# Decoder layer on one core: first batches of the self-attention phase reordered, query-weight low parts moved from VectorE to GpSimd

## What is computed

```python
x = _layernorm(x + self_attention(x))            # causal, 16 heads of 32; q = x @ w_q.T, k = x @ w_k.T, v = x @ w_v.T, out @ w_o.T
x = _layernorm(x + cross_attention(x, context))  # 361 context rows, 16 query heads of 128, 4 key heads, RMS norm of q and k
x = _layernorm(x + mixture(x))                   # top 2 of 8 experts, silu, projection, RMS norm
```

## Time and profile before

| | |
|---|---|
| median of 3 runs | 1489.28 us (1487.9 to 1490.34) |
| the profiled execution, its time | 1489.16 us |
| its span, first to last instruction | 1487.4 us |
| mean granted TensorE clock | 0.977 of full speed |
| PE busy | 1393.6 us (94%) |
| weight loads busy (PEld) | 1176.0 us (79%) |
| DVE busy | 851.4 us (57%) |
| ACT busy | 710.0 us (48%) |
| POOL busy | 594.2 us (40%) |

### The profile page before, as it was taken

One profiled execution on the slowest core, in us unless ns is written; L12 is line 12 of the kernel. 1 busy time (PEld: TensorE's weight loads), 2 busy tenths in 40 slices (PEclk: granted clock), 3 DMA queues, 4 the chain that ended last, 5 costly groups with the idle time before them and its releaser, 6 DMA issues. The chain is left out here.

```text
span 1487.4 us, 24718 instructions
## 1 busy us (share of the span) xinstructions
PE 1393.6 (94%) x8497; PEld 1176.0 (79%) x8497; DVE 851.4 (57%) x3018; ACT 710.0 (48%) x1877; POOL 594.2 (40%) x936
## 2 busy tenths in 40 slices
PE   7889999999987999999999999999999998399996
PEld 6778888887876788888888888888888887277874
DVE  3654343434346676667666765765676665843457
ACT  3655555556325454444444444444454446243346
POOL 1222111212115445455545544554445446264074
PEclk9999999999998999999999999999999999699999
DMA  6211121212443221221222121212221213485372
GB/s 201 91 34 58 56 73 52 79 34 68 142 127 103 76 56 48 65 60 37 67 60 58 35 76 49 68 37 65 59 59 46 65 39 108 175 247 162 114 252 102
DMA packets 70547, 126.56 MB, mean 85 GB/s; under 512 B 11835, under 2 KB 47007, under 8 KB 69528
## 3 DMA queue, kind: packets, MB, share of 16 engines
q1 hardware_dynamic: 65848, 110.04, 24.3%
q0 software_dynamic: 4576, 14.95, 3.6%
HBM read 93.50 MB, written 31.45 MB: 84 GB/s over the span
## 5 line engine op out<-in xcount | busy, mean ns | idle before, releaser
L1363 POOL TENSOR_TENSOR b_pcarry<-b_half 128x1 f32<-128x1 f32 x173 | 43.0, 249 | 364.6 <-DVE b_rinv L1226 343.1
L76 PE MATMUL bank<-b_kTh,b_q 128*100 128x362 f32 x512 | 173.6, 340 | 8.3 <-POOL b_q L1384 5.7
L1106 ACT ACTIVATE b_probs<-b_probs,b_nmax 100x361 f32<-100x361 f32 x256 | 152.4, 595 | 54.7 <-DVE b_nmax L1220 54.6
L1220 DVE CUSTOM_DVE_ANT_0 b_probs<-bank,b_mask 100x361 f32<-100x361 f32 x256 | 135.5, 529 | 69.9 <-issue 61.3
L1395 POOL TENSOR_SCALAR b_probs<-b_probs,b_rinv 100x361 f32<-100x361 f32 x256 | 152.6, 609 | 0.0
L1101 ACT ACTIVATE b_pTh<-bank 121x400 fp32r<-121x400 f32 x192 | 96.1, 501 | 85.1 <-PE bank L937 83.7
L1213 DVE TENSOR_TENSOR b_pTl<-bank,b_pTh 121x400 fp32r<-121x400 f32 x192 | 109.6, 571 | 44.2 <-ACT b_pTh L1101 44.2
L1157 ACT ACTIVATE b_oTh<-bank,b_bv 128x400 fp32r<-128x400 f32 x64 | 38.1, 596 | 198.6 <-PE bank L76 198.6
L937 PE MATMUL bank<-ident,b_probs 100*121 100x100 f32 x768 | 111.7, 268 | 4.1 <-POOL b_probs L1395 3.4
L937 PEld LDWEIGHTS bank<-ident,b_probs 100*121 100x121 f32 x768 | 107.7, 187 | 8.0 <-POOL b_probs L1395 4.4
L436 ACT ACTIVATE a_probs<-a_probs,a_nmax 100x100 f32<-100x100 f32 x256 | 93.1, 366 | 40.3 <-DVE a_nmax L555 40.3
(11 more groups left out here) (256 smaller groups left out, 3818.7 us busy)
## 6 DMA issues: line engine op xcount, KB each, us to landing
q_d<-a_qb SPq DMA_DIRECT2D x64, 200.0 KB, 2.3
b_q_raw<-q_d SPq DMA_DIRECT2D x64, 200.0 KB, 2.4
b_q_raw<-rs_d SPq DMA_DIRECT2D x64, 200.0 KB, 3.4
b_ctxr<-in_ctxT SPq DMA_DIRECT2D x48, 242.0 KB, 4.5
y_d<-c_y SPq DMA_DIRECT2D x32, 256.0 KB, 3.5
c_Eraw<-in_expert_w SPq DMA_DIRECT2D x10, 512.0 KB, 7.8
a_stage<-in_Wq SPq DMA_DIRECT2D x4, 1024.0 KB, 4.9
stage<-in_Wo SPq DMA_DIRECT2D x8, 512.0 KB, 4.5
```

Of the source, the lines that this page charges most:

```text
L76: mm = eng.matmul(out, lhsT=l(c), rhs=r(c), start=first and k == 0, stop=last and k == n - 1)
L1106: act.activation(p, p, ACT.Exp, scale=-1.0, bias=nmax[:, s % 2, h:h + 1], accum_out=psums[:, s % 2, h:h + 1]).then_inc(e_rdy, 1)
L1220: dve.tensor_tensor_reduce(out=probs[:, s % 2, h, 0:SE], in0=s_bank[h % 2][0:S, 0:SE], in1=mask_s[:], scale=-1.0, scalar=BIG, op0=ALU.add, ...
L1363: pool.tensor_tensor(pcarry[:, k:k + 1], half_s[:, 0:1], half_s[:, 0:1], ALU.add)
```

## The change

- The projection for the next pair is cut up in the first batches. In batches 1 to 4 its first half stands ahead of the transposes of x1; in batches 0 to 3 its last quarter stands behind the transposes of the probabilities.
- At the start ACT writes both halves of the scaled queries ahead of the high part of w_o; DVE writes the low part of w_o behind the first masks.
- Each of batches 0 to 3 gets one Wq piece: its high part on ACT (batch 0: behind the output's high part; batches 1 to 3: between the exponentials and x1's high part), its low part on GpSimd at the end of the batch, with a semaphore of its own (wq_lo).
- In even batches before 4, DVE copies the first half of the keys ahead of its copies of the transposed probabilities and the second half behind them.
- wk and wq are laid out in DRAM and SBUF by quarters, so a quarter is one run of 2 KB in each partition; the causal mask is loaded behind both.

```diff
 SQ = 5
-WQ_SPLITS = ((), (2,), (3, 4), (5,))
 KV_FRAME, CTX_FRAME = (50, 52, 59, 61), (48, 50, 57)
...
 
-        wq_s = sb("a_wq", [P, DC, D])
-        wk_s = sb("a_wk", [P, DC, D])
+        wq_s = sb("a_wq", [P, DC, DC, P])
+        wk_s = sb("a_wk", [P, DC, DC, P])
         wvh, wvl = sb("a_wvh", [P, DC, D], F32R), sb("a_wvl", [P, DC, D], F32R)
...
         consts, w_raw, w_hi, w_lo = sem("a_consts"), [sem("a_w_raw0"), sem("a_w_raw1")], sem("a_w_hi"), sem("a_w_lo")
+        wq_lo = sem("a_wq_lo")
         wq_in, wk_in = [[sem(f"a_{w}_in{m}") for m in range(DC)] for w in ("wq", "wk")]
...
             sp.dma_start(xTr[:], xT[0]).then_inc(xT_in, 16)
-            sp.dma_start(causal_s[:], causal).then_inc(causal_in, 16)
             for dst, src, loaded in ((wk_s, w_k, wk_in), (wq_s, w_q, wq_in)):
                 for m in range(DC):
-                    sp.dma_start(dst[:, :, m * P:(m + 1) * P], src[:, :, m * P:(m + 1) * P]).then_inc(loaded[m], 16)
+                    sp.dma_start(dst[:, m], src[:, m]).then_inc(loaded[m], 16)
+            sp.dma_start(causal_s[:], causal).then_inc(causal_in, 16)
             sp.dma_start(qkw_s[:, 0:1], qn_w).then_inc(consts, 16)
...
                 for n in ((2, 3), (4,), (5,))[i] if i < 3 else ():
-                    sp.wait_ge(w_lo, n - 1)
+                    sp.wait_ge(w_lo if n < 4 else wq_lo, (n - 2) % 2 + 1)
                     sp.dma_start(stage[:, n % 2], pieces[n][0]).then_inc(w_raw[n % 2], 16)
...
                         mm = pe.matmul(p_bank(pair, is_q, m // 2)[:, m % 2 * 2 * S:(m % 2 + 1) * 2 * S],
-                                       lhsT=w[:, c, m * P:(m + 1) * P], rhs=xTr[:, c, :], start=c == 0, stop=c == DC - 1)
+                                       lhsT=w[:, m, c, :], rhs=xTr[:, c, :], start=c == 0, stop=c == DC - 1)
                     if m % 2:
...
                 if group == 0 and m % XG == 0:
-                    pe.wait_ge(w_lo, 3 + kv)
+                    pe.wait_ge(wq_lo, 1 + kv)
                 if m >= 2:
...
                 if 1 <= i <= GB:
+                    project(pair + 1, (wk_s, wq_s)[par], range(2), (wk_in, wq_in)[par])
                     transpose_x1(i - 1)
-                if pair + 1 < NPAIR:
-                    project(pair + 1, (wk_s, wq_s)[par], range(DC), (wk_in, wq_in)[par])
+                    project(pair + 1, (wk_s, wq_s)[par], range(2, 3 if i < GB else DC), (wk_in, wq_in)[par])
+                elif pair + 1 < NPAIR:
+                    project(pair + 1, (wk_s, wq_s)[par], range(3 if i < GB else DC), (wk_in, wq_in)[par])
                 elif m[1] is not None:
...
                     mm.then_inc(pt_done, 1)
+                if i < GB:
+                    project(pair + 1, (wk_s, wq_s)[par], range(3, DC), (wk_in, wq_in)[par])
                 if m[2] is not None:
...
                 if b == GB:
-                    act.wait_ge(w_lo, len(pieces))
+                    act.wait_ge(wq_lo, len(pieces) - 2)
                 if b % GB == 0 and b >= 2 * GB:
...
             scaled_q(0, 0)
+            scaled_q(0, 1)
             split_hi(1)
-            scaled_q(0, 1)
             act.wait_ge(half_set, 3)
...
                 exponent(i, 3)
+                if 1 <= i < GB:
+                    split_hi(2 + i)
                 if 1 <= i <= GB:
...
                 act.activation(v_s[:], bank[7][0:S, :], ACT.Copy).then_inc(v_ev, 1)
-                for n in WQ_SPLITS[i] if i < GB else ():
-                    split_hi(n)
                 if i >= GB and par == 1 and pair + 1 < NPAIR:
...
                 act.activation(oTh[:].rearrange("p c t -> p (c t)"), bank[7][:, 0:DC * S], ACT.Copy).then_inc(oT_hi, 1)
+                if i == 0:
+                    split_hi(2)
                 head_squares(m[2])
...
                 if m == 0:
-                    dve.wait_ge(w_lo, len(pieces))
+                    dve.wait_ge(wq_lo, len(pieces) - 2)
                 if m % XG == 0:
...
             split_lo(0)
-            split_lo(1)
-            dve.wait_ge(bq_in, 16)
-            dve.wait_ge(qkw_set, 2)
             for i in range(B):
...
                 elif i == 0:
+                    split_lo(1)
                     invert_sums(i, 0)
...
                     invert_sums(i, 2)
+                    dve.wait_ge(bq_in, 16)
+                    dve.wait_ge(qkw_set, 2)
                 else:
...
                 if i < GB:
-                    for n in WQ_SPLITS[i]:
-                        split_lo(n)
+                    if par == 0:
+                        dve.wait_ge(ks_ev, pair + 1)
+                        copy_k(pair + 1, 0)
                     probs_T(i, 1)
                     probs_T(i, 3)
+                    if par == 0:
+                        copy_k(pair + 1, 1)
                 queries(m[1])
...
                                   oTh[:].bitcast(F32).rearrange("p c t -> p (c t)"), ALU.subtract).then_inc(oT_lo, 1)
-                if pair + 1 < NPAIR:
-                    if par == 0:
-                        if i < GB:
-                            dve.wait_ge(ks_ev, pair + 1)
-                            copy_k(pair + 1, 0)
-                            copy_k(pair + 1, 1)
-                    else:
-                        split_xT(pair + 1)
+                if par == 1 and pair + 1 < NPAIR:
+                    split_xT(pair + 1)
                 queries(m[3])
...
                                    ALU.mult).then_inc(pn_rdy, 1)
+
+            def query_weights_lo(n):
+                pool.wait_ge(w_hi, n + 1)
+                pool.tensor_tensor(pieces[n][2], stage[:, n % 2], pieces[n][1].bitcast(F32), ALU.subtract).then_inc(wq_lo, 1)
 
...
                     keys_in_place(pair + 1)
+                if i < GB:
+                    query_weights_lo(2 + i)
             t = TAIL
...
 
+    def by_output(w):
+
+        return w.reshape(P, w.shape[1], w.shape[2] // P, P).transpose(0, 2, 1, 3)
+
     a = {k: np.asarray(v) for k, v in inputs.items()}
...
         "xT": x.reshape(B // 2, 2, S, DC, P).transpose(0, 4, 3, 1, 2).reshape(B // 2, P, DC, 2 * S),
-        "w_q": chunks(a["L0_attn_w_q"].T),
-        "w_k": chunks(a["L0_attn_w_k"].T),
+        "w_q": by_output(chunks(a["L0_attn_w_q"].T)),
+        "w_k": by_output(chunks(a["L0_attn_w_k"].T)),
         "w_v": chunks(a["L0_attn_w_v"].T),
...
         "Wq": a["L0_xattn_Wq"].reshape(DC, P, XKV, XG * XHD).transpose(2, 1, 0, 3),
```

## The result

The changed kernel took 1477.07 us (median; 1474.73 to 1479.81) beside 1488.59 us (1484.82 to 1490.45) for the kernel before on the same chip: a ratio of 0.9927, interval 0.9905 to 0.9949, or 11.5 us less. The forecast was 1476.7. Three of the six executions took 1474.73 to 1474.86 us with a mean granted clock of 0.980, three took 1479.27 to 1479.81 with 0.976 to 0.977, so the median lies where no execution did.

What follows compares the result with a forecast made beforehand. TensorE was busy nearly throughout, so its waits and half-clock stretches up to batch 4 counted; gains of 4.0 + 2.1 + 2.7 + 2.4 + 1.3 = 12.5 us off 1489.2 gave 1476.7, range 1472.5 to 1482.

Steps and rivals of the forecast that it cites:

- The start: Start to batch 0's product of probabilities and values: that product begins at 30.5 instead of 34.46, gain 4.0 us, bounds 1.9 and 5.3.
- From W: Batch 0, W being w_v's landing at 15.6: scores start near W + 2.9, product of probabilities and values at W + 14.9.
- The 1.0 us put down to the layout: Start: 2 KB runs for wk and wq let w_v land 1.0 us earlier, at 15.6 instead of 16.6.
- The cuts: Batches 1 to 4: cut projections cover PE's waits for x1 and the probability copies; gains 2.1, 2.7, 2.4 and 1.3 us.
- was hidden under the projection and gives nothing: Later batches: taking the 2.3 us query-weight subtraction off DVE saves no time, since the projection already covered it.
- GpSimd's subtraction: End of batches 0 to 3: a query weight's low part takes 4.8 us, bounds 4.4 and 5.6; first ends 8.1 into its step.
- The low part of xT: DVE in batches 1 and 3: beside GpSimd's subtraction this 0.99 us operation ends 1.0 to 1.5 us late, 1.3 taken.
- Rival A: Batches 2 and 4: no conflict between DVE's low part of xT and GpSimd; 1.8 us more gain, 1474.9 us; 15%.
- Rival B: Softmax chain, with ACT's split in it, ends the batches; PE waits 1 us more in three, 1479.7 us; 20%.
- Rival C: Half clock stays at the start and recurs in batches 1 to 4 or later, 1.7 us each; 1479.3 to 1481; 15%.
- Rival D: GpSimd's subtraction holds up every batch's first normalisation in full, 19.2 us against 12.5; slower, 1495.9 us; 3%.
- Rival E: PE's holes only move to the last normalisation, with no net gain over 3 us; 3%.

Runs made afterwards that it cites:

- the two warm-up kernels: Twelve unused 128x128 products ahead of the first projection: on the changed kernel 1477.4 us; with the second and fourth query-weight subtractions also on DVE 1473.53 us.
- the last kernels: Changed kernel with warm-up products, second and fourth subtractions on DVE, ACT's split behind x1's high part: 1475.93 us; also w_v loaded earlier, w_o split later: 1470.43 us.

## Why the prediction was right, and where it was off

**The sum.** 12.5 us were forecast, 12.29 measured at batch 4 and 11.5 between the medians; the time came within 0.4 us. That is luck in two ways. Two errors cancel, the start too high by 1.2 and the steps too low by 1.0; and the median fell between two groups of executions, 2.2 us to either side of it, so no execution came within 1.8 us of the forecast.

**The start was over-priced: 4.0, measured 2.84** (T0 31.62, said to be 30 to 31). Part of this is scatter: the same start gave 2.8 to 3.6 in five kernels, and its order alone, on the old layout, gave 4.03. The step that went wrong is "From W": it let w_v's arrival set the scores' start at W + 2.9. The link itself holds (T0 = W + 14.9 was the forecast, and where w_v is last, as in the two warm-up kernels, it measures 14.75 and 14.76). W came at 15.17, earlier than my 15.6, which by that link gives 30.1. But PE's own two projections ended only at 19.45, and T0 followed 12.17 behind them, the same to 0.02 in the two kernels with the odd subtractions moved (18.65 to 30.82, 19.28 to 31.46) and in that with ACT's split behind x1 (19.40 to 31.58). I had taken PE's end for given because before its projections were over 3.16 us ahead of the scores; I had not asked why the first of them took 7.39 us where the second takes 5.58. By its pace it began at the lower clock, and in after that cost 2.7 us (8.28). With the start's order alone PE's projections ended at 18.32, and there T0 = W + 14.91 (15.52, 30.43), as the forecast's chain has it. The 1.0 us put down to the layout was never there: W scatters from 15.2 to 16.7 with either layout.

**The cuts were right, and under-priced by 0.3, 0.1, 0.3 and 0.2.** T0 to T1 took 15.36 (15.7 forecast), T2 to T3 15.10 (15.4). The waits that I had added in batch 1 (0.3) did not come, and PE's own work in batches 2 and 3 is 15.1 instead of 15.4, as the last kernels' steps show (batch 1's is 15.4). Batch 4's 14.19 was 14.4 in the forecast. No wait stands before L385, as said. What the prediction does not say, and the two halves run alone show, is that neither cuts nor move give more than 0.9 us in the steps by themselves: the sum of terms was right only for both together. That DVE's 2.3 us a piece "was hidden under the projection and gives nothing" held only as long as the projection stood there whole: with the cuts alone it is 8.8 us of waits.

**GpSimd's subtraction**: 4.54 to 4.63 us, 4.8 forecast; the first ended at T0 + 8.0 (39.60 - 31.62), as said.

**The low part of xT**: over 2 us in batches 1 and 3, as said (2.18 each time). It lost 1.19 of the 1.34 us that the two had in common (49.23 to 50.57), where I took 1.3 lost. The Trainium skill, "SBUF — State Buffer", section "Who interferes with whom", would have the second wait for the whole of the first, 1.34 lost: the trace agrees to 0.15 us, and is nearer to it than to the two thirds of the earlier trace rows. Batch 2's step was 16.83 for a forecast of 17.0, with 0.94 us before the fourth transposes (1.2 forecast) and 0.40 before x1's (under 0.7, as said).

**Rival A**, no conflict, falls by the row of 2.18 us. Its price was 1.8; taking the conflict away in fact gave 1.19 in batch 2 and 0.34 in batch 4 (0.61 with the subtraction on DVE). **Rival B**, the softmax chain, was at work in batch 2 alone: moving ACT's split gave back 1.13 us there. I had counted the split in that chain, but not seen that it is enough to remove either link. **Rival C**, the clock: no half clock before 100 us, as said, if the pace of the very first products is left aside. One fell at 1306 to 1311 in the profiled execution, behind a hole of 3.44 us, and its time of 1479.78 is within that rival's 1479.3 to 1481. Three of the six executions lie there or 0.03 us short of it, at a lower mean clock than the other three, so this rival's price, if not its place, was right half the time. Which stretches made those three longer is not shown, since only one of the six was profiled. **Rival D**: only batch 1's first normalisation met the subtraction, and PE did not wait for it. **Rival E** describes each half of the change alone, not the whole.

**Two small slips in the working.** The lower bound of the start's gain is 2.1, not 1.9 (34.46 - 16.6 - 15.8). And by the rule of full exclusion the two low parts would lose 0.2 and 0.3 us more than the 1.3 taken, 0.5 in all and not 0.4. Neither moves the forecast.

## What to carry to other kernels

When work is put ahead of a wait, ask what the next wait then is: here covering 7 us of waits gave 0.9 us until the subtractions in front of the next copies were moved as well, so parts of such a change can't be judged one by one. When a load seems to bound a start, check also that the engine behind it would be ready: compare the durations of alike groups there, since an unlike pair (8.28 and 5.58) points at a limit that the list of waits does not show. And where a whole kernel's time spreads by several us, compare a milestone right behind the change, and see first how far that milestone scatters between kernels that are alike up to it: w_v's arrival did by 1.5 us, and a difference of 1.1 was first read as the layout's.

## What the runs showed of the hardware

- A wait of ACT for one store of the experts' stage is 2.4 to 5.6 us from profile to profile in code that no experiment touched, and with it 105.1 to 110.2 us for the stage.
- A DVE subtraction with two SBUF inputs beside GpSimd's lost nearly all that they had in common (1.19 of 1.34 us); put one behind the other, both took their usual 0.99 and 4.64. With DVE's subtraction first it was GpSimd's normalisation that lost, 1.96 of 2.10 us (2.81 instead of 0.85).
- Bringing the first quarters in runs of 2 KB rather than 512 bytes did not bring PE's first product forward (5.75 against 5.46 before and 5.81 with the old layout; 5.37 to 5.95 over the ten kernels without warm-up); in 4 to 12 us the rate was 315 GB/s against 299.
- The granted clock of the window reads 1.00 in 4 to 12 us while the first projection ran for 8.28 us, at first with 5 products in a microsecond as under a granted 0.50 elsewhere; twelve small products ahead of it made it 5.58.
